# Attention: third pass of a value product as one matmul, and a score tile of 640 keys split as 384 and 256

## The reference

```
q = einsum('bpd,hde->bphe', x, W_Q) + b_Q      # k and v likewise
scores = einsum('bqhe,bkhe->bhqk', q, k) / sqrt(128)
scores = where(causal, scores, -100000.0)
attn = softmax(scores, axis=-1)
z = einsum('bkhe,bhqk->bqhe', v, attn)
out = einsum('bqhe,hed->bqd', z, W_O) + b_O
```

## Time and profile before

| | us | share |
|---|---|---|
| Median of the runs | 1896.71 | |
| Profiled execution, its span | 1896.7 | |
| TensorE matmul busy | 1629.1 | 86% |
| TensorE weight loads busy | 1358.2 | 72% |
| VectorE busy | 1248.5 | 66% |
| ScalarE busy | 973.1 | 51% |
| GpSimd busy | 654.2 | 34% |

### The profile page before, as it was taken

How to read it: one execution, slowest core, us unless ns; L and a number is a source line. 1 busy time by engine, 2 the same in 40 slices (tenths; PEclk the granted TensorE clock), 3 DMA queues, 4 the chain that set the end, 5 groups by cost and what they waited for, 6 DMA issues and landing times.

```text
span 1896.7 us, 31630 instructions
## 1 busy us (share of the span) xinstructions
PE 1629.1 (86%) x9546; PEld 1358.2 (72%) x9546; DVE 1248.5 (66%) x2797; ACT 973.1 (51%) x2046; POOL 654.2 (34%) x725
## 2 busy tenths in 40 slices
PE   3577777888899999999999978999999999658884
PEld 2445444777788788888888877788888888546673
DVE  6677474688965666666666666666666666577564
ACT  3454344445533476666666545566666665433332
POOL 5133336434333333222322123232222221544542
PEclk9789788899999999999999989999999999779897
DMA  3000001200010500000000000000000000422233
GB/s 106 1 1 1 1 1 45 62 17 8 5 21 1 151 23 24 4 19 22 22 22 0 6 18 23 24 24 22 0 22 22 22 6 0 136 71 76 92 113 128
DMA packets 78319, 64.53 MB, mean 34 GB/s; under 512 B 16592, under 2 KB 72640, under 8 KB 78224
## 3 DMA queue, kind: packets, MB, share of 16 engines
q1 hardware_dynamic: 74480, 53.08, 9.7%
q0 software_dynamic: 3744, 10.26, 1.5%
HBM read 44.89 MB, written 18.43 MB: 33 GB/s over the span
## 4 chain that ended last, share of the span: by engine, by line
PE 60%; DVE 16%; issue 7%; DMA 5%; ACT 5%; DVEq 3%; POOL 3%; SPq 1%; POOLq 0%; ACTq 0%
PE psum L53 9%; PE psum L55 9%; PE psum L54 9%; PE psum L1687 6%; DMA moe_results<-moe_y,moe_xrow 4%; PE psum L1700 3%; PE psum L1677 3%; PE psum L1679 3%; PE psum L1678 3%; PE psum L1701 3%; PE psum L1708 3%; DVE table_leaves L589 2%; DVE mamba_conv_sum L1127 2%; DVE mamba_mixed L1149 2%; POOL moe_slots_x L2167 1%
## 5 line engine op out<-in xcount | busy, mean ns | idle before, releaser
L1888 POOL TENSOR_SCALAR attn_probs<-attn_probs,attn_inverse 128x128 f32<-128x128 f32 (+7 forms) x256 | 191.3, 747 | 544.3 <-DVE attn_inverse L1839 544.2
L1756 ACT ACTIVATE attn_pt_hi<-psum 128x512 fp32r<-128x512 f32 (+3 forms) x384 | 185.2, 484 | 183.2 <-PE psum L1687 182.3
L1761 ACT ACTIVATE attn_probs<-attn_probs,attn_neg_max 128x128 f32<-128x128 f32 (+7 forms) x256 | 198.4, 775 | 133.8 <-DVE attn_neg_max L1811 131.6
L1807 DVE TENSOR_TENSOR attn_pt_lo<-psum,attn_pt_hi 128x512 fp32r<-128x512 f32 (+3 forms) x384 | 211.8, 553 | 42.9 <-ACT attn_pt_hi L1756 39.3
L1687 PE MATMUL psum<-ident,attn_probs 128*128 128x128 f32 x1152 | 193.5, 278 | 15.5 <-DVE x_tok L1847 11.9
L1811 DVE CUSTOM_DVE_ANT_0 attn_probs<-psum,attn_mask 128x128 f32<-128x128 f32 (+7 forms) x256 | 192.8, 754 | 20.3 <-PE psum L1679 10.8
L1700 PE MATMUL psum<-attn_pt_hi,attn_v_hi 128*128 128x512 f32 (+3 forms) x384 | 161.2, 420 | 21.8 <-DVE attn_pt_lo L1807 12.5
L1687 PEld LDWEIGHTS psum<-ident,attn_probs 128*128 128x128 f32 x1152 | 139.9, 142 | 40.0 <-issue 12.7
L1677 PE MATMUL psum<-attn_k_hi,attn_q_hi 128*128 128x512 f32 (+3 forms) x384 | 133.8, 348 | 2.6 <-DVE attn_neg_max L1811 2.4
L417 POOL TENSOR_TENSOR gated_h_lo<-gated_hidden,gated_h_hi 128x512 fp32r<-128x512 f32 x56 | 79.6, 1422 | 161.0 <-ACT gated_h_hi L402 161.0
L1701 PE MATMUL psum<-attn_pt_lo,attn_v_hi 128*128 128x512 f32 (+3 forms) x384 | 134.5, 350 | 0.0
(11 more groups left out here) (382 smaller groups left out, 4883.5 us busy)
## 6 DMA issues: line engine op xcount, KB each, us to landing
moe_slots_x<-attn_z_raw SPq DMA_DIRECT2D x2, 2967.0 KB, 17.7
moe_xrow<-moe_slots_x SPq DMA_DIRECT2D x46, 129.0 KB, 2.1
attn_qkv_raw<-in_L_attn_W_Q_dram SPq DMA_DIRECT2D x32, 128.0 KB, 2.2
attn_qkv_raw<-in_L_attn_W_K_dram SPq DMA_DIRECT2D x32, 128.0 KB, 2.4
attn_qkv_raw<-in_L_attn_W_V_dram SPq DMA_DIRECT2D x32, 128.0 KB, 2.5
attn_wo_raw<-in_L_attn_W_O_dram SPq DMA_DIRECT2D x16, 256.0 KB, 3.0
moe_weights_raw<-_L_ffn_gate_up_proj_dram SPq DMA_DIRECT2D x8, 512.0 KB, 5.9
x_in<-_attn_hidden_states_dram SPq DMA_DIRECT2D x4, 512.0 KB, 5.4
```

Source lines behind the costliest of these rows:

```text
L1761: act.activation(probs_view(e), probs_view(e), ACT.Exp, bias=stat(neg_max, e), scale=-1.0, accum_out=stat(sums, e)).then_inc(exp_done, 1)
L1807: dve.tensor_tensor(lo, work_view(e), hi.bitcast(F32), ALU.subtract).then_inc(work_done, 1)
L1888: pool.tensor_scalar(probs_view(e), probs_view(e), stat(inverse, e), 1.0, ALU.mult, ALU.mult).then_inc(probs_ready, 1)
```

## The change

```diff
+    def score_start(e):
+
+        return P if e["t"] == TG else 0
+
     def score_view(e):
         width = (e["t"] + 1) * P
-        slot = 2 * (e["t"] % 2)
-        return s.psum[:, slot:slot + 2, :].rearrange("p b c -> p (b c)")[:, 0:width]
+        slot, at = 2 * (e["t"] % 2), score_start(e)
+        return s.psum[:, slot:slot + 2, :].rearrange("p b c -> p (b c)")[:, at:at + width]
...
                 queries = pair_at(q, slice(None), e["h"], slice(t * P, (t + 1) * P))
-                for at in range(0, (t + 1) * P, GROUP):
-                    end = min(at + GROUP, (t + 1) * P)
+                ends = [*range(GROUP - score_start(e), (t + 1) * P, GROUP), (t + 1) * P]
+                for at, end in zip([0, *ends], ends):
                     (q_hi, q_lo), (k_hi, k_lo) = queries, pair_at(k, slice(None), e["h"], slice(at, end))
...
                 pe.matmul(s.psum[:, 7, at:], v_hi, p_lo[:, at:], start=False, stop=False, skip_group_check=True)
 
-                ends = at + P if j >= TG * e["g"] else at
-                if ends > at:
-                    last = pe.matmul(s.psum[:, 7, at:ends], v_lo, p_hi[:, at:ends], start=False, stop=True,
-                                     skip_group_check=True)
-                if ends < GROUP:
-                    last = pe.matmul(s.psum[:, 7, ends:], v_lo, p_hi[:, ends:], start=False, stop=False, skip_group_check=True)
-                last.then_inc(summed, 1)
+                pe.matmul(s.psum[:, 7, at:], v_lo, p_hi[:, at:], start=False, stop=j >= TG * e["g"],
+                          skip_group_check=True).then_inc(summed, 1)
```

## The result

Four runs of the changed kernel took 1877.94 to 1882.20 us, median 1880.73, beside 1896.70 for the kernel before on the same chip: ratio 0.9918, 95% interval 0.9906 to 0.9931. It is faster by 16 us, where 10.1 were forecast; the time lies 1.6 us under the range's lower end. The profiled execution has a span of 1880.4 us against 1896.7.

What follows compares the result with a forecast made beforehand. TensorE was taken to bound attention. Joined third passes 10.2 us plus score tile 2.9 made 13.1 gross; 3.0 lost in waits left 10.1, so 1896.7 - 10.1 = 1886.6 us, range 1882.3 to 1892.1.

Steps and rivals of the forecast that it cites:

- VectorE's part: VectorE's maximum of the 640-key tile, read across the bank's edge at another place: costed at nothing, bounds 0.05 us a tile.
- rival (c): Longer waits mid-section lower the granted clock; 1.5 us per low-clock stretch, 1908 if all 14 sections got one; chance 0.03.
- Rival (b): A matmul costs only its columns: 192 x 0.01 = 1.9 us, score tile nothing, 0.4 lost: 1895.2 us; chance 0.06.
- Rival (a): ScalarE and VectorE swallow the first head's gain in 13 sections, 4 us more lost: 1890.6 us; chance 0.12.
- the price of the joined passes of key tiles 2 and 6: Attention's value sums: joining 128 + 128 columns into one third pass saves 0.05 us, 0.17 becoming 0.12.
- the two score tiles: The 640-key score tiles, cut 384 and 256 columns: 0.98 to 0.89 us, gain 0.09 each, 2.9 us over 32.
- loss in the middle: TensorE's wait mid-section for ScalarE's z_raw swallows savings before it: 13 sections x 0.10 = 1.3 us lost.
- The ends: Losses in batch 1's first steady section 0.7 us, batch 1's last section 0.6, batch 0's last section 0.4.

Runs made afterwards that it cites:

- The repeat: The changed kernel measured once more, nothing altered: median 1880.84 us, ratio 0.9940 to the kernel before, section 59.00 us.
- The two parts alone: Against the kernel before: only third passes joined, section 59.23 us, ratio 0.9953; only the 640-key score tile recut as 384 and 256, 59.73 us, 0.9976.

## Why the prediction was wrong, point by point

**The direction and the mechanism held.** TensorE bounds the stage; a 128-column matmul in front of a weight load costs 0.05; the widths of 384 and 256 columns took the times read from other tiles; VectorE's part cost nothing; the granted clock stayed 1.00 from 820 to 1100 us, so rival (c) is out. Rival (b) is out by the section (0.93 less, not under 0.15), which does not hang on how starts are recorded. Rival (a) is out too: of the first head 0.38 us are kept (section start to sum 12: 38.00 before, 37.62 after).

**The failed step is the price of the joined passes of key tiles 2 and 6.** The prediction counted up to the start of what follows and gave all three pairs the same 0.05. With 128 + 128 columns the second one is itself too short for the load behind it, so the matmul that follows pays once more: 0.10 for these. By pieces of a section, average of ten: the twelve third passes 0.64 less, the four matmul groups behind key tiles 2 and 6 0.20 less, the two score tiles with the transposes behind them 0.22 instead of 0.18. That is 1.06 us gross where the prediction had 0.82. The kernel with these passes alone measured 0.33 net. With the tile's 0.04 more and the larger loss in the middle, the step is worth 12 x (0.93 - 0.72) = 2.5 us of the whole time: the forecast would have been 1884.1. It alone does not bring the time under the range's 1882.3; the 3.6 us below do.

**The loss in the middle was under-sized by the same mistake.** It is 0.16 us a section and not 0.10: the projection behind c = 10 came early as well and found the same wait. 1.06 - 0.16 = 0.90 is what the pieces explain of the 0.92 to 0.93.

**The ends.** The first section with both heads in batch 1 kept 0.1 us (76.95 before, 76.87 after) and the last section of batch 0 0.2 (76.54 and 76.30). This agrees with the estimates by number only: over the twelve profiles these two sections take 76.5 to 78.1 and 75.5 to 78.9 us, so effects of 0.3 cannot be read from one pair. Twelve turns of the loop make 12 x 0.93 = 11.2 us, and 12.7 were measured from the first score pass to the last sum; the prediction's 10.1 was for this stretch.

**3.6 us lie outside the forecast's stretch.** They lie in code that is the same: 1.5 ahead of attention and 2.1 behind its last sum. In the ten other profiles that were taken the first score pass starts at 650.1 to 652.3 us, and in all twelve the time from the last sum's start to the end is 252 to 257 us, so that the kernels before and after can be two draws of the same thing. That scatter was no part of the range, since the three runs shown agreed within 0.7 us; in the later comparisons the kernel before itself took from 1891.47 to 1899.29 us. This is likely and not shown. The repeat gave 15.0 us in the medians (1895.83 and 1880.84), and its profile has 14.8 us less than before from the first score pass to the last sum instead of 12.7; 1.6 of these 2.1 stand in the first section with both heads of batch 0, and the kernel is the same one. Of the whole gain, 11 us are shown by the loop's turns; where the other 4 to 5 come from, and how much of them is chance, stays open.

**Open.** The two parts alone give 0.66 and 0.16 us a section, together 0.82; the whole change gives 0.93. By the means of all twelve turns it is 0.67 and 0.17, together 0.84, against 0.92, so the gap is 0.08 to 0.11. It stands in no single piece; it is spread over several with 0.02 or less each.

## What to carry to other kernels

Price a short matmul by the distance of starts up to and including the matmul behind it: what its weight load or that of its successor lacks in cover is paid one place later, where a look at the line itself misses it. Cut columns so that every matmul is at least as long as the next load (here 0.11 us, 256 columns and not 128), and change nothing about those that already are. A wait that one engine's queue makes is not filled by moving work into it, if that work needs a buffer or a read from the same queue.

## What the runs showed of the hardware

- An extra matmul with its own weight load costs 0.01 us if both parts are 256 columns wide (0.24 against 0.23), 0.022 with 192 columns, 0.05 with 128, in either order; with 128 columns last the price stands on the successor.
- The 0.11 us do not hang on the matmul's columns, and not every pair of load and matmul has them: matmuls of one column with a 128x128 block are 0.10 us apart, transposes with a block of 8 rows 0.07 (both at a granted clock of 1.00).
- The Trainium skill, "TensorE: Matmul & The Clock Gate", section "LDWEIGHTS (loading the stationary operand)", gives about P/1.2 ns for a load of P columns, an estimate of 107 ns for 128. The trace agrees: 0.11 us between starts of 128-column matmuls in a row, and 0.022 missing with 192 columns. It does so for blocks of 128 rows; with 8 rows and the same 128 columns the starts are 0.07 us apart, less than that formula gives.
- Whole executions of one kernel on one core scattered over 8 us (1891.47 to 1899.29, 24 runs), while a section of its loop repeated within 0.05 us (of the changed kernel within 0.17, over two profiles). An effect of 3 us cannot be read from single executions; the section shows it at once.
